# Six layers of local attention and feed forward: from a loop over layers to one unrolled pipeline of 192 units

## What is computed

```
x = attn_layer(shift_tokens(x), Wqkv[i], q_scale[i], k_scale[i], Wo[i]) + x
x = ffn_layer(shift_tokens(x), ln_g[i], ln_b[i], W1[i], b1[i], W2[i], b2[i]) + x
```

## Time and profile before

| | us |
|---|---|
| median of 3 runs | 5038.49 |
| fastest and slowest of them | 5037.72, 5050.88 |
| span of the profiled execution | 5048.7 |

### The profile page before, as it was taken

The page is one execution under the profiler, slowest core; times in us unless marked ns, Lnnn a source line. Parts: engine busy times, 40 slices in busy tenths (PEclk is TensorE's granted clock), DMA queues, the critical chain, the costliest instruction groups (busy, mean ns, idle before and its releaser), DMA issues. The chain is left out here.

```text
span 5048.7 us, 81560 instructions
## 1 busy us (share of the span) xinstructions
PE 3797.4 (75%) x28548; PEld 2346.0 (46%) x28548; DVE 3273.2 (65%) x6732; ACT 2549.2 (50%) x7024; POOL 2087.9 (41%) x1599
## 2 busy tenths in 40 slices
PE   5288788788789788797778659766666666587897
PEld 2156466466466465564253533333333333355664
DVE  5777476476575575674352643599999999832344
ACT  2199498498597695794121211233333333335443
POOL 0177276375474573671222200266666666500000
PEclk8599899899899899998586878755555555567998
DMA  0011111111111111111000000000000000000000
GB/s 18 28 43 47 36 47 46 36 49 47 36 46 52 30 47 51 34 47 48 0 1 9 1 26 0 0 1 1 1 1 1 1 1 1 1 7 11 12 1 9
DMA packets 48662, 110.09 MB, mean 22 GB/s; under 512 B 8944, under 2 KB 9200, under 8 KB 46704
## 3 DMA queue, kind: packets, MB, share of 16 engines
q1 hardware_dynamic: 48240, 104.66, 6.7%
HBM read 31.23 MB, written 1.05 MB: 6 GB/s over the span
## 5 line engine op out<-in xcount | busy, mean ns | idle before, releaser
L1089 POOL TENSOR_TENSOR slabs<-slabs 128x512 f32<-128x512 f32 x768 | 953.2, 1274 | 379.7 <-DVE slabs L956 322.5
L1786 DVE MAX8 slabs<-slabs 128x8 f32<-128x512 f32 x1084 | 695.1, 686 | 58.3 <-ACT slabs L1723 58.3
L1812 POOL TENSOR_SCALAR slabs<-slabs 128x512 f32<-128x512 f32 x256 | 400.2, 1563 | 470.4 <-DVE slabs L1792 470.4
L1707 ACT ACTIVATE slabs<-slabs 128x512 f32<-128x512 f32 x316 | 212.1, 721 | 727.5 <-DVE slabs L1792 727.5
L859 ACT ACTIVATE slabs<-slabs 128x96 f32<-128x96 f32 x1536 | 556.5, 366 | 19.2 <-PE psum L670 13.3
L1645 PE MATMUL psum<-constants,slabs 128*128 128x128 f32 x1264 | 306.3, 407 | 299.2 <-POOL slabs L1815 298.9
L1788 DVE MATCH_REPLACE8 slabs<-slabs 128x512 f32<-128x512 f32 x768 | 515.5, 683 | 0.0
L623 PE MATMUL psum<-slabs 128*128 128x512 f32 x768 | 411.7, 663 | 128.5 <-DVE slabs L956 63.0
L1078 POOL TENSOR_TENSOR slabs<-slabs 128x768 f32<-128x768 f32 x192 | 282.3, 1470 | 499.1 <-DVE slabs L931 499.1
L1636 PE MATMUL psum<-slabs 8*128 8x512 f32 (+1 forms) x632 | 346.2, 1086 | 164.4 <-ACT slabs L1723 164.1
L1645 PEld LDWEIGHTS psum<-constants,slabs 128*128 128x128 f32 x1264 | 223.3, 209 | 383.4 <-POOL slabs L1815 343.3
(11 more groups left out here) (389 smaller groups left out, 7979.6 us busy)
## 6 DMA issues: line engine op xcount, KB each, us to landing
slabs<-slabs SPq DMA_DIRECT2D x192, 192.0 KB, 2.5
slabs<-slabs SPq DMA_DIRECT2D x192, 128.0 KB, 2.5
slabs<-F1A SPq DMA_DIRECT2D x7, 2176.0 KB, 8.4
slabs<-slabs SPq DMA_DIRECT2D x144, 64.0 KB, 2.1
slabs<-F1F SPq DMA_DIRECT2D x6, 580.5 KB, 4.9
slabs<-S SPq DMA_DIRECT2D x4, 645.0 KB, 5.8
weights<-M SPq DMA_DIRECT2D x1, 2184.0 KB, 9.4
weights<-R SPq DMA_DIRECT2D x2, 1079.5 KB, 5.1
```

Source lines behind the costliest of these rows:

```text
L1089: nc.gpsimd.tensor_tensor(out[:, at, :], normed[u % 2][:, at, :], table, ALU.mult).then_inc(rope_done, 1)
L1786: nc.vector.max(eight, work[side] if k else scores[slot + side]).then_inc(picked[b], 1)
L1812: nc.gpsimd.tensor_scalar(kept[n % 2], scores[slot], tops[:, slot, TOPK - 1:TOPK], None, ALU.is_ge).then_inc(kept_ready, 1)
```

## The change

- `local_layers` takes the place of the loop: one phase, unrolled, with ALL_UNITS = 192 units and 206 steps. The barrier, the clearing of semaphores and the branch between layers are gone; layers are tied by semaphores only. The projection of a sequence waits until that sequence's `finish` of the layer before is done (`shifted_in`).
- Feed forward f (24 of them, 6 layers x 4 sequences) is cut into eight slices, laid into steps 14 + 8f to 21 + 8f (j = 0 to 7). All its products go through one bank (`WIDE`, bank 3). The gate product is copied to SBUF by VectorE (`take_gate`), gelu runs there in place, and the up product comes later into the same bank. There is one set of its buffers. ScalarE changes its table set at j = 5 and back at j = 6: 48 loads of a set in place of 12.
- Weights and rotary tables have two homes (a new SBUF tensor, `annex`, and space in `weights`). SyncE issues the next layer's attention weights ahead of unit 10's moves and its feed forward weights ahead of unit 14's. The feed forward weights of layer 0 join the first load.
- q and k are apart from projection to normalisation: square, sum and normalise run on 512 columns twice. VectorE adds rope k of unit i - 2 at the start of a step and rope q of unit i - 1 at its end (q first, k second before).
- v and the weighed context share bank 2, the output product moves to the tail of bank 4, behind the scores. `copy_values` moves ahead of the squares on ScalarE, and the first half of the transposes of probabilities ahead of `weigh` on TensorE.

```diff
-    W = m.slab(2, 3)[:, 0:width]
-    for_attention = W[:, 0:offsets(F1_ATTENTION)[1]]
-    for_forward = W[:, offsets(F1_ATTENTION)[1]:width]
+    attention_width = offsets(F1_ATTENTION)[1]
+    W = [m.slab(2, 3)[:, 0:width], m.annex[:, 0:width]]
...
-    with nc.Fori(0, F1_LAYERS) as layer:
-        local_layer(nc, m, ins, layer, w, for_attention, for_forward, angles, tables, shifted, qT, hA, hB)
+    local_layers(nc, m, ins, w, scale_tables, for_attention, for_forward, tables, shifted, hA, hB)
...
+    def forward_at(i):
+
+        f, j = divmod(i - 14, 8)
+        return (f, j) if 0 <= f < FORWARDS else (None, None)
...
-            for u in range(UNITS):
+            for u in range(U):
                 b, t, half = place(u)
+                layer, n = divmod(u, UNITS)
+                if n == 10 and layer + 1 < F1_LAYERS:
+                    if layer >= 1:
+                        sp.wait_ge(out_product, UNITS // 2 * layer)
+                    sp.dma_start(for_attention[(layer + 1) % 2], ins["F1A"][layer + 1]).then_inc(attention_loaded[(layer + 1) % 2], 16)
+                if n == 14 and layer + 1 < F1_LAYERS:
+                    if layer >= 1:
+                        sp.wait_ge(down_added, BATCH * layer)
+                    sp.dma_start(for_forward[(layer + 1) % 2], ins["F1F"][layer + 1]).then_inc(forward_loaded[(layer + 1) % 2], 16)
...
             def project(u):
                 b, t, half = place(u)
-                if u >= 1:
-                    pe.wait_ge(unit_normed, u)
+                layer = layer_of(u)
+                if u % UNITS == 0:
+                    attention_ready(pe, layer)
+                if layer >= 1 and t == 0 and half == 0:
+                    pe.wait_ge(shifted_in, 2 * (BATCH * (layer - 1) + b) + 2)
                 tokens = shifted[:, b, REACH + t * P:REACH + t * P + P]
                 for i, name in enumerate(("q", "k")):
-                    last = nc.tensor.matmul(ps[:, i, :], tokens, w(name, 512 * half, 512), start=True, stop=True)
-                last.then_inc(qk_product, 1)
+                    if u >= 1:
+                        pe.wait_ge(unit_normed, 2 * u - 1 + i)
+                    nc.tensor.matmul(ps[:, i, :], tokens, w(layer, name, 512 * half, 512), start=True, stop=True).then_inc(qk_product, 1)
...
-                pe.wait_ge(v_copied, min(u + 3, UNITS))
+                pe.wait_ge(masked_step, MAX_STEPS * min(u + 3, U - 1) + 1)
...
+            def up_gate(f, c):
+                pe.wait_ge(biased, f + 1)
+                if c:
+                    pe.wait_ge(gate_taken, 3 * f + c)
                 rows = FF1_ROWS[c]
...
-                if i < UNITS:
+            for i in range(STEPS):
+                f, j = forward_at(i)
+                if i < U:
                     project(i)
-                if 0 <= i - 2 < UNITS:
+                if j == 4:
+                    up_gate(f, 1)
+                if j == 7:
+                    up(f, 2)
+                if 0 <= i - 2 < U:
                     turn_queries(i - 2)
-                if 0 <= i - 5 < UNITS:
+                if 0 <= i - 4 < U:
+                    turn_probs(i - 4, 0)
+                if 0 <= i - 5 < U:
                     weigh(i - 5)
-                if 0 <= i - 4 < UNITS:
-                    turn_probs(i - 4, 0)
-                if 0 <= i - 2 < UNITS:
+                if 0 <= i - 2 < U:
                     turn_keys(i - 2)
-                if 0 <= i - 6 < UNITS and i % 2 == 1:
+                if j == 0:
+                    centre(f)
+                if j == 1:
+                    variance(f)
+                if j == 2:
+                    spread(f)
+                if j == 3:
+                    up_gate(f, 0)
+                if j == 4:
+                    up_gate(f, 2)
+                if j == 5:
+                    up(f, 0)
+                if j == 6:
+                    up(f, 1)
+                if 0 <= i - 6 < U and i % 2 == 1:
                     project_out(i - 6)
-                if 0 <= i - 4 < UNITS:
+                if 0 <= i - 4 < U:
                     turn_probs(i - 4, 1)
-                if 0 <= i - 2 < UNITS:
+                if 0 <= i - 2 < U:
                     score(i - 2)
-                if 0 <= i - 3 < UNITS:
+                if 0 <= i - 3 < U:
                     values(i - 3)
...
+                if j == 7:
+                    down(f)
...
-            def square(u):
-                act.wait_ge(qk_product, u + 1)
+            def square(u, side):
+                act.wait_ge(qk_product, 2 * u + side + 1)
                 if u >= 1:
-                    act.wait_ge(root_step, ROOT_STEPS * (u - 1) + 1)
-                nc.scalar.activation(squares, QK, ACT.Square).then_inc(squared, 1)
+                    act.wait_ge(root_step, ROOT_STEPS * (u - 1) + side + 1)
+                nc.scalar.activation(squares[:, side, :, :], QK[side], ACT.Square).then_inc(squared, 1)
...
+            for i in range(STEPS):
+                f, j = forward_at(i)
+                if 0 <= i - 4 < U:
+                    copy_values(i - 4)
+                if i < U:
+                    square(i, 0)
+                    square(i, 1)
+                if 0 <= i - 2 < U:
                     copy_queries(i - 2)
-                if 0 <= i - 4 < UNITS:
-                    copy_values(i - 4)
-                if i < UNITS:
+                if j == 6:
+                    gelu(f, 1)
+                    gelu(f, 2)
+                    if f < FORWARDS - 1:
+                        nc.scalar.preload_act_table_set("natural_log_exp_and_others")
+                if i < U:
                     root_of_sum(i)
-                if 0 <= i - 4 < UNITS:
+                if j == 3:
+                    bias(f)
+                if 0 <= i - 4 < U:
                     copy_probs(i - 4, 0)
-                if 0 <= i - 2 < UNITS:
+                if 0 <= i - 2 < U:
                     copy_keys(i - 2)
-                if 0 <= i - 5 < UNITS:
+                if 0 <= i - 5 < U:
                     copy_context(i - 5)
-                if 0 <= i - 3 < UNITS:
+                if 0 <= i - 3 < U:
                     exponential(i - 3)
-                if 0 <= i - 4 < UNITS:
+                if j == 5:
+                    nc.scalar.preload_act_table_set("gelu_and_others")
+                if 0 <= i - 4 < U:
                     copy_probs(i - 4, 1)
...
+                if j == 0:
+                    square_centred(f)
+                if j == 5:
+                    gelu(f, 0)
...
-            def sum_squares(u):
-                dve.wait_ge(squared, u + 1)
-                nc.vector.tensor_reduce(sums, squares, axis=AX.X, op=ALU.add).then_inc(root_step, 1)
+            def sum_squares(u, side):
+                dve.wait_ge(squared, 2 * u + side + 1)
+                nc.vector.tensor_reduce(sums[:, 8 * side:8 * side + 8], squares[:, side, :, :], axis=AX.X, op=ALU.add).then_inc(root_step, 1)
...
+            def take_gate(f, c):
                 rows = FF1_ROWS[c]
+                dve.wait_ge(gate_product, 3 * f + c + 1)
+                nc.vector.tensor_copy(hidden[c][0:rows, :], WIDE[0:rows, :]).then_inc(gate_taken, 1)
...
+            def finish(f):
+                b = f % BATCH
+                dve.wait_ge(down_product, f + 1)
+                nc.vector.scalar_tensor_tensor(out=hA[:, b, 1:PADSEQ], in0=WIDE, scalar=w(f // BATCH, "b_down"),
                                                in1=hB[:, b, 1:PADSEQ], op0=ALU.add, op1=ALU.add).then_inc(down_added, 1)
-                dve.wait_ge(down_added, b + 1)
+                dve.wait_ge(down_added, f + 1)
                 for rows, start in ((slice(0, 64), 1), (slice(64, P), 0)):
-                    nc.vector.tensor_copy(shifted[rows, b, REACH:STRIP], hA[rows, b, start:start + SEQ])
-
...
+            for i in range(STEPS):
+                f, j = forward_at(i)
+                if 0 <= i - 2 < U:
+                    rope(i - 2, 1, k_roped)
+                if 0 <= i - 4 < U:
                     total(i - 4)
+                if 0 <= i - 3 < U:
                     mask_scores(i - 3)
+                if j == 0:
+                    shift(f)
+                if j == 2:
+                    variance_roots(f)
+                if j == 4:
+                    take_gate(f, 1)
+                if j == 6:
+                    gated(f, 0)
+                if i < U:
+                    sum_squares(i, 0)
+                    sum_squares(i, 1)
                     measure(i)
+                if 0 <= i - 3 < U:
                     find_maxima(i - 3)
+                if 0 <= i - 6 < U and i % 2 == 1:
                     residual(i - 6)
+                if i < U:
                     refine(i)
+                    normalise(i, 0)
+                    normalise(i, 1)
+                if j == 2:
+                    scale(f)
+                if j == 3:
+                    take_gate(f, 0)
+                if j == 4:
+                    take_gate(f, 2)
```

(10 more changed lines are left out.)

387 lines of the change are left out of this document (138 added, 249 removed).

## The result

The changed kernel takes 5240.32 us (median of 4, 5235.79 to 5242.52), the kernel before 5038.27 beside it: 1.0394 times as long, interval 1.0379 to 1.0409. It is slower; 78 us less were forecast, 202 more came.

A forecast was written before the change was run, and what follows sets the result against it. ScalarE (94% busy), TensorE and a ring of waits were nearly tight. Layers of 124 + 1856 + 47 + 75 = 2055 against 2145 us (-90), load +2, clock +10: -78, so 4960 us from 5038.5; range 4800 to 5070.

The forecast's parts named there:

- the pattern of the slices: Eight steps carrying one feed forward beside the units: 83.4 us, bounds 70.9 to 71.2 (work alone) and 89.5.
- The plain step: Step with a unit and no slice: 8.45 us, mean of 8.17 and 8.7 in odd steps.
- j1, j3, j5, j7: Feed forward steps with square and copy, bias, nothing extra, and down product at the end: 9.15, 8.82, 8.17, 8.17 us.
- j2: Feed forward step with the variance root on VectorE between mask and sums, 2.5 us with waits: step 11.3 us.
- j0: Step where VectorE stands at `finish` for the down product, with copies, mask and sums queued behind: 14.4 us.
- The clock: TensorE slowing behind holes at j0, j2 and j6: 0.4 us per feed forward, 10 us in all.
- Rival B: Holes at j0, j2 and j6 keep TensorE at 1.2 GHz in every feed forward: 5190 us, chance 0.13.
- The load at the start: First phase also loads layer 0's feed forward weights, 580 KB beside 2784 KB: 2.3 us more.
- j6: Feed forward step with two table loads and three gelus on ScalarE, some from the end of j5: 12.4 us.
- C: Rival: weight loads hold up value moves, TensorE waits in `weigh`: 5045 us, no change; chance 0.07 together with D.
- D: Rival: the unrolled form overlaps nothing, layers stay at 357 us; chance 0.07 together with C.
- A: Rival: stalls are absorbed and only ScalarE's work counts: 4690 us, half absorbed 4825; chance 0.25.

The follow-up runs named there:

- order_back: Changed kernel with weigh again ahead of the first transposes of the probabilities on TensorE: 5191.57 us, ratio 1.0306.
- before_swap: Kernel before with only the first transposes of the probabilities moved ahead of weigh on TensorE: 5133.23 us, ratio 1.0188.
- odd_late: Changed kernel with variance, first gate and first up products (j1, j3, j5) moved behind the second transposes: 5162.01 us, ratio 1.0240.
- roots_early: Changed kernel with the variance root moved from j2 to the end of j1, where GpSimd has not begun: 5167.79 us, ratio 1.0257.
- extra_roots: Kernel before with three more variance roots per layer on unread scratch columns, while GpSimd rotates: 5188.91 us, ratio 1.0301.
- fill_all: Changed kernel with products whose result is overwritten put into TensorE's holes of j0, j2 (both) and j6: 5201.72 us, ratio 1.0289.
- no_loads: Changed kernel with gelu replaced by the identity and the slices' 47 table-set loads left out: 5164.11 us, ratio 1.0245.
- together: Changed kernel with weigh first, root at j1's end, odd-step slices behind second transposes, down behind next projection, finish behind maxima, earlier shift copies: 4930.57 us, ratio 0.9795.
- together2: Kernel of together with centre behind the scores, down behind the keys' turning, up and gate of j4 and j7 behind the queries' turning: 4892.50 us, ratio 0.9708.

## Why the prediction was wrong

The forecast of the layers was 2055 us, the trace has 2337.6: 283 more, the whole miss. By its terms: the first 14 steps 119.5 (225.1 to the 14th normalisation at 344.56) instead of 124, although the plain pair was longer: the 6 for a slow start didn't come, as the first two intervals were 7.25 and 7.57 where before has 9.00; the 178 steps 2125.4 instead of 1856; the tail 92.8 instead of 75, within its bounds of 60 and 95. The step of the prediction that failed is the pattern of the slices, 83.4 us for 8 steps where 95.5 came, above its upper bound of 89.5 too, together with the plain step under it.

- *The plain step*, "8.45; bounds 8.17 and 8.7". The short steps were 8.21, as said; the long ones 9.46, outside the bounds. The step followed ScalarE to "the next unit's last exponential" and let nothing hold the exponentials. It left out that they wait for the second transposes of the unit before, and thus all of TensorE's order ahead of these. The exchange of first transposes and weigh was told among the changes and then given no price. Before, weigh filled the time until GpSimd's probabilities came, so that no wait for them stood in the trace; the exchange uncovers it. order_back (8.46) and before_swap (+96 us) show it. With that wait gone the longer step is the even one (8.61, and 8.31 for the odd one), the one behind the residual, as the forecast had argued. Its sign for this, the first 14 steps more than 0.3 from 8.45 on average, didn't warn: they average 8.67, as the pipeline's first intervals are short, while the steady pair was 0.39 off.
- *j1, j3, j5, j7* (9.15, 8.82, 8.17, 8.17 against 10.2, 12.3, 10.2, 10.9) miss by 9.2 us in sum. In each of them the exponentials idle for the transposes, 1.02, 2.05, 2.06 and 1.20 us. odd_late takes 2.6 off the first three (to 9.7, 10.7 and 9.7); with all four orders j3 and j5 come to 8.6 and 8.5.
- *j2*: "2.5 with its waits". It is 6.9. The price was read from the feed forward behind the pipeline, where GpSimd is idle (11.99 us busy of 87.4); the slices lie beside its rotations. roots_early and extra_roots show it. GpSimd's work was read for its length and never for what it does to VectorE, of which L949 at 385.53 was a sign. The same holds of the shift copies at j0: 2.50 against the 0.87 that was counted. j0 came out at 15.2 for 14.4 nonetheless, and that is partly luck. The wait for `finish` was seen rightly but priced too high: `finish` starts 1.8 after the exponentials (1300.99 to 1302.80) instead of 3.3, and from there to the end of the sums (1309.84) it is 7.0 instead of 5.5. Both give the 8.9 of the forecast.
- *The clock*, "I take 0.4" within bounds of 0 and 3 a feed forward: filling the holes in fill_all brought 1.7 (mean of 8 steps 95.54 and 93.85; 1.6 by the medians, 2.2 by the ratios). Rival B named the mechanism and the places rightly, j0, j2 and j6, after which the grant is 0.84 to 0.90 in four of eight steps. But B's point of decision, 3.3 us, was not reached, and that its 5190 stands nearest to the 5240 is luck. Its sign, a mean grant over the layers below 0.9, was a poor one: the mean was 0.92 and hid it.
- *The load at the start*, "+2.3": it costs 0.07 (11.14 us for 11.07 from issue to scaling). That the layers began 2.2 later came from the stage ahead of it, and is less than traces with the same start differ by.
- *Right*: the restarts are gone; j6 12.4 (12.4 said); no load of weights is waited for (C); what remains of the unrolled form does overlap (against D). j4 was priced too high (11.0, 9.8); which of its terms wasn't followed up. A, absorbed stalls, is refuted: ScalarE is busy 1684.1 of 2337.6 us.
- *The tables*: the Trainium skill (ScalarE: Activation LUTs, "What ACT_TABLE_LOAD costs") was weighed with a drain, 2.66 in all. The trace disagrees: the next operation starts within 0.02 us of a load's end, and the whole cost is 1.62 (no_loads). The forecast was right to leave the drain out.

That VectorE is held is a rule of the Trainium skill too (SBUF — State Buffer, "SBUF: two separate sides"): VectorE and GpSimd share a pair of ports as an exclusive lock, which VectorE wants for operations with two inputs in SBUF and for its two-port fast modes. The trace agrees in kind: the root's operations and the 64 x 512 copies are held, while the mask (one input in PSUM, 0.92) and the two sums (one input, 1.28 for both at 1308.56, while GpSimd ran) are not. Had the rule been applied to each operation that the change moves, the root and the copies would have been dearer by (6.9 - 2.3) + (2.50 - 0.87) = 6.2 us in each feed forward, by the durations of after. At 22.25 x 6.2 = 138 us that would have turned the 78 less into some 60 more: an estimate, which takes both as being on the path.

What stays open: how the 310 us of together divide among its four orders, since their effects don't add, and why j4 rises in together2.

## What to carry to other kernels

When calls are reordered, look for the wait that lets the next user write over a buffer, and follow it through the whole queue of the engine that frees it; one exchange of two calls cost 96 us here. Read the duration of a small VectorE operation from a stretch in which GpSimd does what it will do beside it, since it can be seven times as long. In a pipeline with several stalls, repair them together: one at a time gains little, as the next one takes over, and the same slices went from 4% slower to 3% faster than before by order alone.

## What the runs showed of the hardware

- A VectorE operation of 4 columns that reads SBUF lasts until the GpSimd operation beside it ends, 1.18 instead of 0.16 us, each anew (j2 of after, extra_roots); two copies of 64 x 512 took 2.50 us instead of 0.87. GpSimd itself was not slowed by the root (4.93 us for four), and little by the copies (5.32).
- In after TensorE worked at its lower level behind holes of 1.98 (j0), 3.78 and 1.32 (j2) and 2.67 us (j6): scores took 1.56 for 0.89, v 2.07 for 1.12. From the grants (length x 2 x (1 - grant)) that was 3.3 us at j0, 2.9 + 3.9 at j2 and j3, 3.5 at j7. Holes of 1.60 in the plain steps of before left the grant at 1.00. Filling the holes with products that nobody reads brought 39 us.
